# A quantized feed-forward kernel: where x and the weights are loaded from, the order of the weight turns, and when int16 becomes bf16

## What is computed

```python
mask = arange(512) < length[b]
y = (causal_conv(x * mask, kernel[h]) + x * mask * D[h]) * mask
q = clip(round(y * sqrt(7) / (mean|y| + eps)), -8, 7)          # per row of 512
w_q(w) = clip(round(w / (mean|w| + eps)), -1, 1)               # gate, up: 1376x512; down: 512x1376
inter = int8_quant((q @ w_q(up).T) * relu(q @ w_q(gate).T)**2) # per row of 1376
out = x + inter @ w_q(down).T                                  # scales left out here
```

## Time and profile before

| | |
|---|---|
| median of 3 runs | 234.68 us (233.23 to 234.84) |
| the profiled execution | 234.12 us |
| its span, first to last instruction | 232.3 us |
| mean granted TensorE clock | 0.978 of full speed |
| busy: PE (TensorE) | 182.3 us, 78% |
| busy: DVE (VectorE) | 159.6 us, 69% |
| busy: ACT (ScalarE) | 117.5 us, 51% |
| busy: POOL (GpSimd) | 30.5 us, 13% |
| moved by DMA | 34.39 MB |

### The profile page before, as it was taken

How to read it: one execution, slowest core, us unless ns; L and a number is a source line. 1 busy time by engine, 2 the same in 40 slices (tenths; PEclk the granted TensorE clock), 3 DMA queues, 4 the chain that set the end, 5 groups by cost and what they waited for, 6 DMA issues and landing times.

```text
span 232.3 us, 3346 instructions
## 1 busy us (share of the span) xinstructions
PE 182.3 (78%) x1083; PEld 93.1 (40%) x1083; DVE 159.6 (69%) x424; ACT 117.5 (51%) x189; POOL 30.5 (13%) x76
## 2 busy tenths in 40 slices
PE   1007099994598986879898989898988989898893
PEld 1004085762145532334444444453534434343352
DVE  6996047350846798987768595959577776868762
ACT  0185475643657899180908263553628081623730
POOL 8135899400000000000000000000000000000000
PEclk9999999999689999799999999999999999999999
DMA  5879493598241999869762826453554433451514
GB/s 180 330 325 279 112 299 75 130 351 232 65 112 42 246 170 208 195 129 245 153 170 56 199 81 140 105 120 113 107 140 84 82 71 74 104 110 43 107 35 103
DMA packets 45695, 34.39 MB, mean 148 GB/s; under 512 B 37646, under 2 KB 37934, under 8 KB 44654
## 3 DMA queue, kind: packets, MB, share of 16 engines
q1 hardware_dynamic: 44718, 31.55, 55.5%
q10 hardware_dynamic: 800, 2.62, 3.4%
q0 software_dynamic: 160, 0.00, 0.0%
HBM read 21.07 MB, written 4.28 MB: 109 GB/s over the span
## 4 chain that ended last, share of the span: by engine, by line
PE 59%; DMA 13%; ACT 11%; DVE 8%; issue 5%; POOL 1%; ACTq 1%; DVEq 0%; POOLq 0%
PE down_ps L630 12%; PE gate_ps L593 12%; PE up_ps L598 9%; DMA raw<-in_L_ffn_w_up_dram 9%; PE conv_ps L513 8%; PE tr_dve_ps L513 6%; DMA q_int<-y_int 4%; PE conv_ps L630 3%; ACT g L755 3%; DVE i_t L1053 3%; DVE inter L1076 3%; PE tr_act_ps L499 2%; ACT int L698 2%; PE down_ps L513 2%; ACT x_t L712 1%
## 5 line engine op out<-in xcount | busy, mean ns | idle before, releaser
L755 ACT ACTIVATE g<-gate_ps,gu_scale 128x416 f32<-128x416 f32 (+2 forms) x48 | 30.5, 636 | 73.2 <-PE gate_ps L593 73.2
L1076 DVE SCALAR_TENSOR_TENSOR inter<-up_ps,gu_scale,g 128x416 f32<-128x416 f32 (+2 forms) x48 | 33.3, 695 | 22.3 <-ACT g L758 20.3
L598 PE MATMUL up_ps<-up_t,q_t 128*128 128x416 bf16 (+2 forms) x192 | 45.4, 359 | 4.1 <-DVE inter L1076 4.1
L593 PE MATMUL gate_ps<-gate_t,q_t 128*128 128x416 bf16 (+2 forms) x192 | 45.1, 357 | 0.1
L630 PE MATMUL down_ps<-down_t,i_t 128*128 128x512 bf16 (+1 forms) x132 | 30.6, 380 | 11.1 <-DVE i_t L1053 11.1
L1080 DVE TENSOR_REDUCE imax<-inter 128x1 f32<-128x416 f32 (+2 forms) x48 | 30.3, 631 | 1.7
L758 ACT ACTIVATE g<-g 128x416 f32<-128x416 f32 (+2 forms) x48 | 28.1, 586 | 1.5
L598 PEld LDWEIGHTS up_ps<-up_t,q_t 128*128 128x128 bf16 x192 | 18.6, 98 | 23.0 <-DVE inter L1076 4.9
L593 PEld LDWEIGHTS gate_ps<-gate_t,q_t 128*128 128x128 bf16 x192 | 17.6, 98 | 16.0 <-issue 2.5
L630 PEld LDWEIGHTS down_ps<-down_t,i_t 128*128 128x128 bf16 (+1 forms) x132 | 11.9, 98 | 29.1 <-DVE i_t L1053 16.4
L513 PE MATMUL conv_ps<-toep,x_t 128*64 128x512 f32 (+3 forms) x128 | 20.9, 473 | 3.1 <-ACT x_t L712 3.1
(11 more groups left out here) (179 smaller groups left out, 220.4 us busy)
## 6 DMA issues: line engine op xcount, KB each, us to landing
toep<-k_back SPq DMA_DIRECT2D x16, 512.0 KB, 4.2
out_dram<-o_sb SPq DMA_DIRECT2D x30, 128.0 KB, 2.7
raw<-in_x_dram SPq DMA_DIRECT2D x6, 512.0 KB, 6.9
raw<-in_L_ffn_w_down_dram SPq DMA_DIRECT2D x2, 1376.0 KB, 10.1
raw<-in_L_ffn_w_gate_dram SPq DMA_DIRECT2D x1, 1536.0 KB, 10.1
raw<-in_L_ffn_w_up_dram SPq DMA_DIRECT2D x1, 1536.0 KB, 17.6
raw<-in_L_ffn_w_gate_dram ACTq DMA_DIRECT2D x1, 1024.0 KB, 5.1
x_first<-in_x_dram SPq DMA_DIRECT2D x2, 512.0 KB, 21.6
```

Source lines behind the costliest of these rows:

```text
L593: mm = pe.matmul(gate_ps[bank][:, 0:cn], q_t[m % 3][:, i, :], gate_t[:, i, c0:c0 + cn], start=(i == 0), stop=(i == KB - 1))
L598: mm = pe.matmul(up_ps[bank][:, 0:cn], q_t[m % 3][:, i, :], up_t[:, i, c0:c0 + cn], start=(i == 0), stop=(i == KB - 1))
L755: nc.scalar.activation(g2[bank][:, 0:cn], gate_ps[bank][:, 0:cn], ACT.Relu, scale=gu_scale[m % 4][:, 0:1]).then_inc(relu_done, 1)
L1076: v.scalar_tensor_tensor(out=inter[:, c0:c0 + cn], in0=up_ps[bank][:, 0:cn], scalar=gu_scale[m % 4][:, 1:2], in1=g2[bank][:, 0:cn], op0=AL ...
```

## The change

- Up's and gate's tails are issued ahead of their 1024 KB; x quad 0 goes to ScalarE's queue behind up's load; D's load goes to GpSimd's queue.
- x quad 1 and down's weights are issued by ScalarE between its copies, x quads 2 and 3 by GpSimd behind its tables. SyncE issues none of these any more.
- The turns go in the order in which the products' column chunks need them, with their own list of banks; products(0, 0) waits for the first eight only; the copies are shared out anew. Rounding of gate's two parts is swapped between ScalarE and VectorE, and the sums of part 1 go before those of part 0.
- Two clock matmuls fewer; conv(3) stands behind products(0, 1).
- i_cast(n) stands at the end of the slot before the one of down(n).

```diff
--- before.py
+++ after.py
@@ -71,8 +71,9 @@
-        TURNS = (3, 4, 5, 0, 1, 2, 6, 7, 8, 9, 10, 11)
-        COPY_ACT, COPY_DVE = (0, 1, 4, 6, 8, 11), (2, 3, 5, 7, 9, 10)
+        TURNS = (0, 1, 6, 7, 2, 8, 3, 9, 4, 10, 5, 11)
+        TURN_BANK = (0, 1, 2, 3, 0, 1, 2, 3, 1, 3, 1, 3)
+        COPY_ACT, COPY_DVE = (2, 3, 4, 8, 10, 11), (0, 1, 5, 6, 7, 9)
...
@@ -273,7 +274,7 @@
             c0, c1 = 2 * g * P, min((2 * g + 2) * P, I)
-            bank = wt_ps[i % 4][:].bitcast(I16).rearrange("p (k c) -> p k c", k=KB)
+            bank = wt_ps[TURN_BANK[i]][:].bitcast(I16).rearrange("p (k c) -> p k c", k=KB)
             return (gate_t, up_t)[m][:, :, c0:c1], bank[:, :, 0:c1 - c0]
...
@@ -281,6 +282,10 @@
+        def turned_before(i):
+            return max((j for j in range(i) if TURN_BANK[j] == TURN_BANK[i]), default=None)
...
@@ -319,8 +324,14 @@
             else:
+                eng.dma_start(raw[m][0:IR, WIDE, :], w[WIDE * P:I, :]).then_inc(w_loaded[m][1], 16)
                 eng.dma_start(raw[m][:, SPLIT:WIDE, :], full[:, SPLIT:, :]).then_inc(w_loaded[m][1], 16)
-                eng.dma_start(raw[m][0:IR, WIDE, :], w[WIDE * P:I, :]).then_inc(w_loaded[m][1], 16)
+        def load_quad(eng, q):
+            for half in range(2):
+                h0 = head_of(4 * q, half)
+                eng.dma_start(x_quad[q][half_rows(half), :],
+                              x[:, h0:h0 + 4, :].rearrange("b h s -> b (h s)")).then_inc(x_loaded[q], 16)
...
@@ -329,15 +340,8 @@
-            def load_quad(q):
-                for half in range(2):
-                    h0 = head_of(4 * q, half)
-                    sp.dma_start(x_quad[q][half_rows(half), :],
-                                 x[:, h0:h0 + 4, :].rearrange("b h s -> b (h s)")).then_inc(x_loaded[q], 16)
...
             load_inner(sp, 1, w_up, 0)
-            load_quad(0)
...
@@ -354,17 +358,8 @@
                 load_toep(n)
-            for i in range(2):
-                sp.wait_ge(w_rounded[1][i], 1)
-            load_quad(1)
             store_k(1)
             load_toep(4)
-            for i in range(2):
-                sp.wait_ge(w_rounded[0][i], 1)
-            down_rows = w_down.rearrange("(c p) i -> p c i", p=P)
-            for i in range(2):
-                s = weight_part(2, i)
-                sp.dma_start(raw[2][s], down_rows[s]).then_inc(w_loaded[2][i], 16)
...
@@ -399,13 +394,9 @@
                     load_toep(m + 5)
-                if m == 1:
-                    load_quad(2)
                 if m in (2, 3):
...
                     turn_down(2 * m - 3)
-                if m == 4:
-                    load_quad(3)
             for n in DOWNS[T - 1]:
...
@@ -427,6 +418,13 @@
+            pool.wait_ge(pool_zeros, 1)
+            for g in range(2):
+                row = g * JR + JA - 1
+                pool.dma_start(d_tail[row:row + 1, :, JB - 1],
+                               Dskip[g * HG:(g + 1) * HG].rearrange("(a h) -> a h", a=1),
+                               allow_slow_non_contiguous=True).then_inc(d_loaded, 16)
...
@@ -470,6 +468,13 @@
+            for i in range(2):
+                pool.wait_ge(w_rounded[1][i], 1)
+            load_quad(pool, 2)
+            for i in range(2):
+                pool.wait_ge(w_rounded[2][i], 2)
+            load_quad(pool, 3)
...
@@ -526,9 +531,9 @@
                 pe.wait_ge(w_rounded[m][0 if 2 * g + 2 <= SPLIT else 1], 1)
-                if i >= 4:
-                    pe.wait_ge(*copied(i - 4))
-                bank = wt_ps[i % 4][:].bitcast(BF16).rearrange("p (k c) -> p k c", k=KB)
+                if turned_before(i) is not None:
+                    pe.wait_ge(*copied(turned_before(i)))
+                bank = wt_ps[TURN_BANK[i]][:].bitcast(BF16).rearrange("p (k c) -> p k c", k=KB)
                 for c in range(2 * g, min(2 * g + 2, IB)):
...
@@ -560,10 +565,10 @@
             turn(1)
+            xt(1)
             turn(2)
-            xt(1)
             turn(3)
-            keep_clock(4)
+            keep_clock(2)
             conv(0)
...
@@ -572,22 +577,22 @@
             turn(7)
+            turn(8)
             xt(3)
-            turn(8)
-            conv(2)
             first_q()
             turn(9)
+            conv(2)
             turn(10)
             turn(11)
-            conv(3)
...
                 if m == 0:
-                    pe.wait_ge(w_dve_copied, len(COPY_DVE))
-                    pe.wait_ge(w_act_copied, len(COPY_ACT))
+                    last = 8 if c == 0 else len(TURNS)
+                    pe.wait_ge(w_dve_copied, sum(i < last for i in COPY_DVE))
+                    pe.wait_ge(w_act_copied, sum(i < last for i in COPY_ACT))
                 wait(pe, relu_done, NC * m + c - 1)
...
@@ -646,6 +651,8 @@
                 products(m, 1)
+                if m == 0:
+                    conv(3)
                 if m == 1:
...
@@ -668,13 +675,8 @@
             load_inner(act, 0, w_gate, 1)
-            act.wait_ge(pool_zeros, 1)
-            for g in range(2):
-                row = g * JR + JA - 1
-                act.dma_start(d_tail[row:row + 1, :, JB - 1],
-                              Dskip[g * HG:(g + 1) * HG].rearrange("(a h) -> a h", a=1),
-                              allow_slow_non_contiguous=True).then_inc(d_loaded, 16)
             load_inner(act, 1, w_up, 1)
+            load_quad(act, 0)
...
@@ -726,23 +728,31 @@
             nc.scalar.activation(warm[:], averaging[:, 0:1], ACT.Abs)
+            weight_sum(0, 1)
             weight_sum(0, 0)
-            weight_sum(0, 1)
+            weight_sum(1, 1)
             weight_sum(1, 0)
-            weight_sum(1, 1)
             xt_copy(0)
-            weight_round(0, 0)
-            weight_copy(0)
+            weight_round(0, 1)
             xt_copy(1)
-            weight_copy(1)
+            weight_copy(2)
+            weight_copy(3)
             weight_copy(4)
+            for i in range(2):
+                act.wait_ge(w_rounded[1][i], 1)
+            load_quad(act, 1)
             xt_copy(2)
             y_sum(0)
-            weight_copy(6)
+            weight_copy(8)
             y_round(0)
+            act.wait_ge(w_rounded[0][0], 1)
+            down_rows = w_down.rearrange("(c p) i -> p c i", p=P)
+            for i in range(2):
+                s = weight_part(2, i)
+                act.dma_start(raw[2][s], down_rows[s]).then_inc(w_loaded[2][i], 16)
             xt_copy(3)
-            weight_copy(8)
             y_sum(1)
+            weight_copy(10)
             weight_copy(11)
...
@@ -1023,29 +1033,27 @@
             k_copy(0)
-            weight_round(0, 1)
+            weight_round(0, 0)
             weight_mean(1)
             weight_round(1, 0)
-            weight_copy(2)
-            weight_copy(3)
+            weight_copy(0)
+            weight_copy(1)
             weight_round(1, 1)
...
                                         op0=ALU.mult, op1=ALU.mult))
+            weight_copy(5)
             y_mask(0)
-            weight_copy(5)
             k_copy(1)
+            weight_copy(6)
             y_scale(0)
...
             y_scale(1)
-            weight_copy(10)
             y_mask(2)
-            y_mask(3)
-            q_copy(1)
...
@@ -1088,9 +1096,9 @@
                 gated(1)
-                for n in DOWNS[m]:
-                    if n < T - 2:
-                        i_cast(n)
+                if m == 0:
+                    y_mask(3)
+                    q_copy(1)
                 if m == 1:
...
@@ -1123,6 +1131,10 @@
                     down_copy(1)
+                if m + 1 < T:
+                    for n in DOWNS[m + 1]:
+                        if n < T - 2:
+                            i_cast(n)
                 for n in DOWNS[m]:
...
                         out_add(n)
```

## The result

The changed kernel takes 220.64 us (median of 4 runs, 219.80 to 221.38) beside 234.76 us for the kernel before (233.23 to 235.61): ratio 0.940, 95% interval 0.935 to 0.946. The forecast was 214.5 us, so 14.1 us came of the 20 expected. The profiled execution took 220.53 us, its span 218.7.

The account below looks back on a forecast made before the run. Bound by up's weights, the stretch from mean to first product, q's transpose in slot 0, then TensorE with conversion breaks; 10.7 + 0.9 + 4.8 + 3.2 + 0.3 = 19.9 us off 234.12 gave 214.2, predicted 214.5, range 209.5 to 222.

Parts of the forecast that it names:

- Conversions: Slots 4 to 15: casting a slot ahead removes TensorE's waits before the down products, 9.2 us in all.
- The term for slots 5 to 11: Steady slots: the wait of 0.69 us before the down product goes in each of seven slots, 4.8 us.
- the 1.0 charged for that: Slot 4: x quad 3, loaded in slot 3, makes down's transposes land 1.0 us late, between nothing and 3.4.
- rival C: Slot 0: q's transpose starves beside down's load and x quad 2, landing 6.2 us late; 221 us, chance 0.10.
- The mean at 22.8: Start: up's weights land and are summed sooner, so the second mean's matmuls start at 22.8 against 28.54, 5.7 us gained.
- Rival B: Start: up's last piece comes late whatever the order, sums end at 28.0, 5.2 us later; 219.7 us, chance 0.14.
- From the mean to the first product: Second mean to first product: 20.7 us against 22.04, including a new 2.7 us wait before first_q, without the clock charge.
- The 1.5 us for the clock: Before the first product: the new wait may lower TensorE's clock, charged at 1.5 us (0 to 3.5).
- Slot 0: Slot 0 takes 10.75 us against 15.85, q of tile 1 landing at 55.1, before slot 1 begins at 55.75.
- A: Whole kernel: the forecast's main case, 214.5 us, its own range 209.5 to 218, chance 0.64.
- D: Slots 4 to 15: another wait replaces the removed one in each slot, so 9.2 us don't come; 223.7 us, chance 0.07.
- E: TensorE: the wait before first_q sets off a low clock lasting for slots, some 7 us more each; 237 us, chance 0.03.

## Why the prediction was right and wrong

**Conversions: right, and too small.** I had 9.2 us for slots 4 to 15; the changed kernel's windows show 11.8 (1.7 + 7 x 0.86 + 4.1), the edit alone 12.5, helped by slot 3's 1.4 us of clock, of which its slot 4 gives 0.8 back. The term for slots 5 to 11 took the wait of 0.69 in the earlier trace rows and left TensorE's 10.04 busy; the slot came out at 9.87. The missing 0.17 lies in the down group itself: from the end of the product before it (111.60 by TensorE's timeline) to the next convolution (113.90) it now takes 2.30 us, against 3.17 before, of which 0.69 were the wait and so 2.48 the group. I read this as the start of the first matmul behind a gap, so that a wait costs a little more than its length; no run tries that by itself. In slot 4 `down_copy` ends 5.43 us into the slot in both kernels (103.10 - 97.67; 99.76 + 1.66 - 95.99). So x quad 3 did not delay it, the 1.0 charged for that did not come, and 1.7 of the possible 1.87 went. The risk was real all the same: VectorE waited for down's transposes for 1.8 us in the profile with the old order of sums and for 1.5 in the one with the tails last. (The 6.9 us of the earlier trace rows that this term and rival C use is a median, not an upper bound.)

**The mean at 22.8: wrong, it came at 27.44.** Two steps failed, and 0.4 is a slip: the sum came to 23.2 and went on as 22.8. The first is "landed some 0.9 later, at 20.2": 5.64 MB over the measured rate gives when the bytes are through, but up's ScalarE share landed at 22.2, and in every kernel whose x stood behind up on ScalarE's queue, or came later, the last piece came at 21.5 to 22.5, whichever piece it was. That is 2.0 us; what sets the time of the landing stays open. The second is that I let the 2.95 us of the long sum alone follow; as the piece that lands last is the one that is summed first, 5.2 us follow. That is 2.3, and the old order of the sums gives them back. Rival B had both (28.0 for the end of the sums, 27.39 measured). What the old kernel lost there I had named correctly as x, beside the rest of up: 3.9 us by the run that puts it back.

**From the mean to the first product: right in sum.** 20.7 predicted without the clock, 20.71 measured. The wait was 1.85 for 2.7 us, because I put the DMA issues of down in series with ScalarE's work. The 1.5 us for the clock did not come in the changed kernel (1.00 in its window), but did in the profile with the old sums.

**Slot 0: wrong, rival C.** The step that failed is "may delay the transpose as long as before at no cost". 10.75 us were right for TensorE's own pace (11.06 once x quad 2 was out of the way or behind down). But I looked only at q of tile 1, with the landing of before, when x quad 2 was not yet on its way. toep(4), a plain load that landed in 4.2 us before, took 16.3, and the wait for it brought the half-speed convolution that I had charged elsewhere. C had the mechanism and nearly the price (6.2 for 5.6), but named q's transpose, which landed 0.3 us behind toep(4), and not toep(4). I gave it 0.10, on the ground that TensorE's pace left time, which is no statement about how the landing itself grows.

**The sum.** 4.6 us lost at the mean and 5.9 in slot 0; 1.5 of clock not charged, 1.2 more in slots 5 to 11, 0.8 in slot 4 and 0.6 in the tail: 19.9 - 4.6 - 5.9 + 1.5 + 1.2 + 0.8 + 0.6 = 13.5, the difference of the two profiled executions (234.12 - 220.53 = 13.6). I had treated B and C as alternatives; both came, with 10.5 us together, and 4.1 us that I had not expected from slot 4 on and from the clock made up for part of it. That the time lies within the range is luck to that extent. Two slips changed little: the low end of A's range adds up to 210.05, not 209.5, and 214.2 with the 0.56 is 214.8, not 214.5. D and E did not occur.

## What to carry to other kernels

Before moving a load to an idle queue, list what else is in flight in that stretch and which load the next stage waits for: here a third queue made that load land 4.4 us later than two did. Putting the big loads behind one another on one queue avoided it, and summing the pieces in the order in which they land started the next stage 3.0 us sooner. A cheap operation that stands last before TensorE's next group costs the wait that it causes and a little more, once a slot (0.69 and 0.17 us here), and moving it was the edit with the most certain gain.

## What the runs showed of the hardware

- x on a third queue, GpSimd's, cost more than its bytes. With the same loads issued by 49 us, three queues moved 242 GB/s from 49 to 57 us and two 281; toep(4) took 16.3 us to land against 11.9, 9.7 with x held back, and 4.2 in the kernel before, where down's load was issued behind it. The Trainium skill (DMA: Bandwidth & Descriptors, "Issuing engines are not separate DMA queues") says that another issuing engine gives no bandwidth; these runs agree, and show besides that it can slow a load on another queue.
- A DMA issue on ScalarE's queue costs its compute nothing while a longer operation runs (0.92 us of issues, wait before first_q unchanged at 1.85), but where the issues outlast the work they leave a gap: 0.84 us behind four in a row, and 1.19 us in the changed kernel behind the two of x quad 1, which took 2.05 us.
- The low clock is not tied to one length of gap: behind the same wait of 1.85 us the convolution took 2.38 us at 1.00 (2.4 GHz) in the changed kernel and 3.92 in the one with x held back and the old sums, whose window from 42.39 to 45.80 has 0.50 (1.2 GHz); behind 2.80 us it took 4.06. In slot 3, behind 2.43 us, it took 3.78 in the changed kernel and 2.38 in the one with the conversions alone. What decides between them stays open. The window, columns as in the earlier trace rows:

```profile
42.39:45.80 3.41, 3.41 (x18) 1.46 (x15) 0.61 (x5) 0.00 (x0) 1.71 (x4) 0.50 1.01 410
```
